# Routing tokens to experts batch by batch: token numbers scattered into fixed ranges of a table in memory, read back by one gather

## What is computed

```python
x = x + attn(cond(x, itok))        # a linear map chosen per batch, then causal attention with 16 heads of 16
h = cond2(x, itok)                 # two linear layers with relu and low-rank terms, per batch
gate_weights = softmax(h @ gate_w + gate_b, axis=-1)         # 8 experts
topk_vals, topk_idx = top_k(gate_weights, 2)
e = gelu(h @ w1[n] + b1[n]); e = gelu(e @ w2[n] + b2[n]); expert_out[n] = e @ w3[n] + b3[n]
out = x + sum over the two chosen n of topk_vals * expert_out[n]
```

## Time and profile before

| | us |
|---|---|
| median of 3 runs | 1474.47 (1473.1 to 1475.62) |
| the profiled execution | 1473.53 |
| its span, first to last instruction | 1471.8 |
| TensorE busy | 1299.8 (88%) |
| VectorE (DVE) busy | 814.7 (55%) |
| ScalarE (ACT) busy | 682.5 (46%) |
| GpSimd (POOL) busy | 515.0 (35%) |
| mean granted clock of TensorE | 0.940 of full |

### The profile page before, as it was taken

The page is one execution under the profiler, slowest core; times in us unless marked ns, Lnnn a source line. Parts: engine busy times, 40 slices in busy tenths (PEclk is TensorE's granted clock), DMA queues, the critical chain, the costliest instruction groups (busy, mean ns, idle before and its releaser), DMA issues.

```text
span 1471.8 us, 26713 instructions
## 1 busy us (share of the span) xinstructions
PE 1299.8 (88%) x8313; PEld 974.7 (66%) x8314; DVE 814.7 (55%) x1753; ACT 682.5 (46%) x1301; POOL 515.0 (35%) x809
## 2 busy tenths in 40 slices
PE   5878989988988988989989885459899999999997
PEld 3436656656656656656666554448788888888886
DVE  4626646646646646556556433745455555555553
ACT  4654654655655655655655630023333333333332
POOL 0332332332332432432332420324354444544442
PEclk9579999999999999999999978569999999999998
DMA  5112223222232132132132223733525224242220
GB/s 176 44 48 89 83 77 116 79 85 96 80 123 87 64 122 82 65 123 87 55 113 79 80 86 129 292 137 73 217 43 155 36 43 141 52 148 38 38 43 11
DMA packets 50765, 137.54 MB, mean 93 GB/s; under 512 B 10658, under 2 KB 29730, under 8 KB 49026
## 3 DMA queue, kind: packets, MB, share of 16 engines
q0 software_dynamic: 28992, 68.35, 16.4%
q1 hardware_dynamic: 21698, 68.18, 12.8%
HBM read 86.03 MB, written 51.38 MB: 93 GB/s over the span
## 4 chain that ended last, share of the span: by engine, by line
PE 71%; DVE 11%; ACT 8%; DMA 3%; issue 3%; POOL 3%; SPq 0%; POOLq 0%; DVEq 0%; ACTq 0%
PE bank L691 65%; PE bank L973 4%; DVE nmax L1359 4%; ACT q_sb L1160 3%; ACT probs_t L1153 2%; PE bank L965 1%; DVE hid_low L1286 1%; DMA xg<-hrows,gid 1%; POOL w_rest L1617 1%; ACT ot_sb L1169 1%; DMA out<-y_sb,sid 1%; POOL wsplit L1621 1%; PE bank L893 1%; DVE mm_sb L1366 1%; ACT sums L1170 1%
## 5 line engine op out<-in xcount | busy, mean ns | idle before, releaser
L1359 DVE TENSOR_REDUCE nmax<-bank 128x1 f32<-128x512 f32 (+3 forms) x512 | 221.4, 485 | 120.7 <-PE bank L691 120.4
L1153 ACT ACTIVATE probs_t<-bank 128x512 f32<-128x512 f32 (+1 forms) x384 | 181.1, 524 | 119.8 <-PE bank L691 119.3
L1193 ACT ACTIVATE g<-z 128x512 f32<-128x512 f32 x142 | 89.8, 632 | 280.6 <-DVE z L1555 280.6
L1603 POOL TENSOR_SCALAR_AFFINE_SELECT probs_t<-probs_t 128x256 f32<-128x256 f32 x256 | 97.8, 406 | 336.3 <-ACT probs_t L1153 336.1
L691 PE MATMUL bank<-wst,g1t_high 128*128 x568 | 185.7, 408 | 0.9 <-DVE g1t_low L1543 0.9
L1665 POOL DMA_INDIRECT out<-y_sb,sid x71 | 114.4, 1611 | 152.1 <-DVE y_sb L1576 69.0
L1617 POOL TENSOR_TENSOR w_rest<-w_rest,w_high 128x512 f32<-128x512 f32 x64 | 82.0, 1282 | 173.5 <-ACT w_high L1039 173.5
L1555 DVE TENSOR_TENSOR z<-bank,b_sb 128x512 f32<-128x512 f32 x142 | 98.2, 692 | 73.3 <-PE bank L691 62.6
L691 PEld LDWEIGHTS bank<-wst,g1t_high 128*128 128x128 f32 x568 | 102.6, 191 | 20.6 <-issue 1.1
L691 PE MATMUL bank<-wst,g1t_low 128*128 x284 | 113.1, 398 | 0.0
L691 PE MATMUL bank<-wst,g2t_high 128*128 x568 | 108.4, 291 | 1.5 <-DVE g2t_low L1543 1.5
(11 more groups left out here) (223 smaller groups left out, 2879.4 us busy)
## 6 DMA issues: line engine op xcount, KB each, us to landing
wst<-wsplit SPq DMA_DIRECT2D x8, 4096.0 KB, 12.5
w_rest<-in_w_all POOLq DMA_DIRECT2D x64, 256.0 KB, 2.9
wsplit<-w_high POOLq DMA_DIRECT2D x64, 256.0 KB, 2.3
wsplit<-w_rest POOLq DMA_DIRECT2D x64, 256.0 KB, 2.5
hrows<-h_sb SPq DMA_DIRECT2D x8, 528.0 KB, 4.0
x_in<-in_xT SPq DMA_DIRECT2D x8, 512.0 KB, 3.7
wb_raw<-in_lora_wb SPq DMA_DIRECT2D x8, 512.0 KB, 3.5
x1t<-in_xT SPq DMA_DIRECT2D x8, 512.0 KB, 4.3
```

What stands on the lines that cost most here:

```text
L1153: taken(nc.scalar.activation(probs_t[:, (2 * g + half) % PT_SLOTS, S * u:S * u + width], at(n, rd)[:, 0:width], ACT.Exp), n, rd)
L1193: nc.scalar.activation(g[:, :], z[:, :], ACT.Gelu).then_inc(s_g, 1)
L1359: ins = V.tensor_reduce(nmax[:, g % 2, half, i:i + 1], at(n, rd)[:, cols], AX.X, ALU.max, negate=True)
L1603: ins = nc.gpsimd.affine_select(diag, diag, [[0, 2], [1, P]], ALU.is_ge, 0.0, base=0, channel_multiplier=-1)
```

## The change

Routing is spread over the rounds. A table id_table in memory has a fixed range of 4096 places for each of the 8 experts, filled with the number 4096 (no token) at the start. In round n, DVE takes the logits of batch n - 2 (`pick`, step 24): top two, one-hot masks. TensorE counts within the batch with five matmuls (product "pre", step 26). DVE adds the running count of each expert (route_sb) and gets each token's place in the table (`give_slots`, step 27, slot_id). POOL scatters the 512 token numbers twice, for first and second choice, by eight indirect DMAs of 128 numbers of 4 bytes (`put`), three behind the load of piece 5, three behind that of 6, two behind that of 7. In round 8 slots are given for batch 6 and at its end for batch 7; their 16 puts stand at the end of the rounds. DVE computes from the counts how many tiles each expert has and which row of 128 places of the table each tile is (block_id); one indirect DMA gathers these rows (ids_t), one transpose and one copy make ids, used for gathers and scatters alike. slot_id has one buffer: DVE writes it only when all puts of the batch before have landed. The copy into logits, the one-hot products and their constants go. Every expert has at least one tile and they run in the order 0 to 7, so SP loads the weights of experts 0, 1 and 2 in round 8 (`load_run`), and the biases after them, ahead of the last hrows. `product` "pre" takes a bank of the filler ring, so the fillers after it change banks.

```diff
-HIT_GROUP = NT // 4
+CAP = B * S
+PUTS = 2 * TB
+PICK_STEP, PRE_STEP = 24, 26
+PUT_WITH = {5: (0, 3), 6: (3, 6), 7: (6, PUTS)}
...
+        if routes and step == PRE_STEP:
+            take(("pre", 0), "filler")
...
+    if not attends:
+        take(("pre", 1), "filler")
...
+    id_table = nc.dram_tensor("id_table", [NE * CAP, 1], F32, kind="Internal").ap()
...
+            def load_run(r):
+                sp.wait_ge(s_wsplit, 32 * W_PIECES * (r + 1))
+                if r >= 1:
+                    sp.wait_ge(s_w, 16 * r)
+                sp.dma_start(wst[:, (1 - r) % W_SLOTS, :, :].bitcast(F32),
+                             wsplit[r:r + 1, :, :, :].rearrange("o p h n -> (o p) h n")).then_inc(s_w, 16)
+
             def turn(rd, last=False):
+                if rd.b is None:
+                    filled(sp, ("ks", HEADS // 2 - 1), Round(rd.p))
+                    sp.dma_start(tile_sb[:, :], tile_c).then_inc(s_tile_c, 16)
+                    filled(sp, ("pv", QUADS - 1), Round(rd.p))
+                    load_run(0)
...
+                    if rd.b is None:
+                        load_run(1)
+                        for n in x1s:
+                            filled(sp, n, rd)
+                        load_run(2)
+                        filled(sp, ("h", TB - 1), rd)
+                        load_bias()
...
+            sp.dma_start(tri_f[:, :], tri).then_inc(s_const, 16)
...
+            sp.dma_start(route_sb[:, :], route_c).then_inc(s_mid, 16)
+            sp.dma_start(id_table.rearrange("(n p) o -> n (p o)", p=P), pads).then_inc(s_pads, 16)
...
-            sp.wait_ge(s_wsplit, 32 * NE * W_PIECES)
-            sp.wait_ge(s_runs, 1)
-            for r in range(NE):
-                e_run = sp.value_load(run_e[0:1, r:r + 1], min_val=0, max_val=NE - 1)
...
+            sp.wait_ge(s_ends, 1)
+            for r in range(W_SLOTS, NE):
+                v_end = sp.value_load(run_end[0:1, r - W_SLOTS:r - W_SLOTS + 1], min_val=0, max_val=TILES)
+                v_out = sp.snap(v_end + before_c[BL3])
+                sp.wait_ge(full[BL3], v_out)
+                sp.sem_inc(s_tick, 1)
+                load_run(r)
...
+                elif what == "pre":
+                    vacant(pe, n, rd)
+                    pe.wait_ge(s_hots, (p if m else rd.routed) + 1)
+                    mm(dst()[:, 0:TB * NE], tri_b[:, :], hots[:, :, :].rearrange("p t e -> p (t e)"),
+                       start=True, stop=False, skip_group_check=True)
+                    for t in range(TB):
+                        later = TB - t
+                        ins = mm(dst()[:, (t + 1) * NE:(TB + 1) * NE].rearrange("p (t e) -> p t e", e=NE),
+                                 ones_b[:, :], hots[:, t, :].unsqueeze(1).to_broadcast([P, later, NE]),
+                                 start=False, stop=(t == TB - 1), skip_group_check=True)
...
-            for n in range(2 * NT // HIT_GROUP):
-                pe.wait_ge(s_hit_r, n + 1)
-                pe.wait_ge(s_hit_v, n + 1)
-                for t in range(HIT_GROUP):
-                    ins = mm(bank[ID_BANK][:, 0:TW], hit_r[:, n % 2, t, :], hit_v[:, n % 2, t, :],
-                             start=(n == 0 and t == 0), stop=(n == 2 * NT // HIT_GROUP - 1 and t == HIT_GROUP - 1))
-                ins.then_inc(s_hitu, 1)
-
-            pe.wait_ge(s_route, 1)
+            product(Round(B), ("pre", 1))
+            pe.wait_ge(s_ids_t, 16)
+            pe.wait_ge(free[ID_BANK], before_b[ID_BANK] + 1)
+            nc.tensor.transpose(bank[ID_BANK][:, 0:TW], ids_t[0:TW, :], id_f[0:TW, 0:TW]).then_inc(full[ID_BANK], 1)
...
+                        nc.scalar.copy(tri_b[:, :], tri_f[:, :])
...
+            def pick(q):
+
+                dve.wait_ge(s_gchain, q * 3 + 1)
+                weight = route_sb[:, 0:NE].unsqueeze(1).to_broadcast([P, TB, NE])
+                for c, (src, most) in enumerate(((glog, gmax), (lg2, top))):
+                    if c == 1:
+                        link(V.tensor_reduce(top[:, :], lg2[:, :, :], AX.X, ALU.max))
+                    link(V.tensor_tensor(rk[:, c, :, :], src[:, :, :], over_e(most[:, :]), ALU.is_equal))
+                    link(V.tensor_tensor(rk[:, c, :, :], rk[:, c, :, :], weight, ALU.mult))
+                    link(V.tensor_reduce(top[:, :], rk[:, c, :, :], AX.X, ALU.max))
+                    link(V.tensor_tensor(hot[:, c, :, :], rk[:, c, :, :], over_e(top[:, :]), ALU.is_equal))
+                    if c == 0:
+                        link(V.scalar_tensor_tensor(lg2[:, :, :], hot[:, 0, :, :], -BIG, glog[:, :, :], ALU.mult, ALU.add))
+                V.tensor_tensor(hots[:, :, :], hot[:, 0, :, :], hot[:, 1, :, :], ALU.add).then_inc(s_hots, 1)
+
+            def give_slots(rd, m):
+
+                n, q = ("pre", m), rd.p if m else rd.routed
+                filled(dve, n, rd)
+                begun = route_sb[:, NE:2 * NE]
+                link(V.tensor_tensor(pre[:, :, :], at(n, rd)[:, 0:TB * NE].rearrange("p (t e) -> p t e", e=NE),
+                                     begun.unsqueeze(1).to_broadcast([P, TB, NE]), ALU.add))
+                taken(V.tensor_tensor(begun, begun, at(n, rd)[:, TB * NE:(TB + 1) * NE], ALU.add), n, rd)
+                drained(dve, n, rd)
+                link(V.tensor_tensor(rk[:, :, :, :], hot[:, :, :, :],
+                                     pre[:, :, :].unsqueeze(1).to_broadcast([P, 2, TB, NE]), ALU.mult))
+                link(V.tensor_reduce(slot[:, :, :], rk[:, :, :, :], AX.X, ALU.add))
+                if q:
+                    dve.wait_ge(s_id_put, 16 * PUTS * q)
+                V.tensor_copy(slot_id[:, :, :], slot[:, :, :]).then_inc(s_put, 1)
...
-                    V.tensor_copy(logits[:, bass.ds(p * TB, TB), :], glog[:, :, :])
...
+                if b is None:
+                    pick(p)
                 if p is not None:
                     for n_fill, piece in rd.fillers(STEPS - 1):
                         take(rd, n_fill, piece)
+                if b is None:
+                    give_slots(rd, 1)
...
+            V.tensor_scalar(block_id[:, :], block_f[:, :], own, None, ALU.add).then_inc(s_block, 1)
...
+            V.tensor_copy(ids[:, :], bank[ID_BANK][:, 0:TILES]).then_inc(free[ID_BANK], 1)
...
+            def put(q, first, last):
+
+                if q < 0:
+                    return
+                if first == 0:
+                    pool.wait_ge(s_put, q + 1)
+                    if q == 0:
+                        pool.wait_ge(s_pads, 16)
+                for i in range(first, last):
+                    t, c = divmod(i, 2)
+                    nc.gpsimd.indirect_dma_start(
+                        id_table, bass.IndirectOffsetOnAxis(ap=slot_id[:, c, t:t + 1], axis=0),
+                        route_sb[:, 2 * NE + q * TB + t:2 * NE + q * TB + t + 1], None,
+                        bounds_check=NE * CAP - 1, oob_is_err=False).then_inc(s_id_put, 16)
...
                     load_piece(b, piece)
+                    if piece > IN_STEPS:
+                        put(b - 2, *PUT_WITH[piece])
                     split_piece(b, piece)
...
+            for q in (B - 2, B - 1):
+                put(q, 0, PUTS)
+            pool.wait_ge(s_block, 1)
+            pool.wait_ge(s_id_put, 16 * PUTS * B)
+            nc.gpsimd.indirect_dma_start(
+                ids_t[0:TW, :], None, id_table.rearrange("(n p) o -> n (p o)", p=P),
+                bass.IndirectOffsetOnAxis(ap=block_id[0:TW, 0:1], axis=0),
+                bounds_check=NE * CAP // P - 1, oob_is_err=False).then_inc(s_ids_t, 16)
```

More of the change, by code:

```diff
@@ L385, in build_kernel @@
+        starts = sb("starts", [1, TILES, NE - 1], F32)
+        expert_f = sb("expert_f", [1, TILES], F32)
+        turns = sb("turns", [1, 2, TILES], F32)
+        place = sb("place", [1, 2, TILES], F32)
         xg = sb("xg", [P, 2, ROW], F32)
@@ L896, in turn @@
                         product(rd, n_fill, piece)
+                    if step == PRE_STEP and rd.routed is not None:
+                        product(rd, ("pre", 0))
                     if quad is not None:
@@ L1386, in turn @@
                         take(rd, n_fill, piece)
+                    if rd.routed is not None and step == PICK_STEP:
+                        pick(rd.routed)
+                    if rd.routed is not None and step == PRE_STEP + 1:
+                        give_slots(rd, 0)
                     if step in LOW_STEPS:
@@ L1499, in _ @@
[L1499 to L1503 removed]
+            link(V.tensor_scalar(past[:, :], tbase[:, 1:NE + 1], own, None, ALU.is_le))
@@ L1651, in gather @@
             def gather(j, vj1, buffer):
[L1652 removed]
+                nc.gpsimd.tensor_copy(gid[:, :], ids[:, bass.ds(j, 1)]).then_inc(s_gid, 1)
                 pool.wait_ge(s_gid, vj1)
```

344 lines of the change are left out of this document (112 added, 232 removed).

## The result

| | us |
|---|---|
| changed kernel, median of 4 runs | 1511.07 (1505.58 to 1515.7) |
| before, 4 runs beside them | 1475.05 (1473.1 to 1476.27) |
| ratio | 1.0232, 95% interval 1.0204 to 1.0259: slower |
| profiled execution, its span | 1511.56, 1509.8 |

The prediction was 1451 with a range of 1436 to 1467, and 0.08 for slower.

What follows compares the result with a forecast made beforehand. TensorE, busy 88% of the span, was held up by a 66.0 us stretch without overlap before the expert stage. 1473.5 - 25.8 (tail) + 3.6 (rounds) = 1451.3, about 1451 us; range 1436 to 1467.

Steps and rivals of the forecast that it cites:

- The hole and its place: Between last gate (904.60) and first transpose of gathered rows (970.57), 66.0 us without overlap, which the change should shorten.
- The price of a put on POOL: POOL's time per put, c: taken as 1.61 us, between 1.07 and 2.46, plus 0.85 once a group.
- The landing of the puts: End of the rounds: batch 6's puts land 4.1 us after issue beside loads, batch 7's 2.05 us.
- POOL in the rounds: Openings of rounds: three puts take 5.7 us against piece 5's slack of 6.68 or 3.91; load 6 late, + 1.5 us.
- The rest of the rounds: TensorE's five matmuls + 2.4 us, dropped logits copy - 0.6, ScalarE's tri cast and SP's constants at the start + 0.3.
- The bound of 0 for TensorE's five matmuls: Rounds 2 to 7: lower bound if TensorE waits nearby anyway; 0.4 us each taken, upper bound 0.6.
- The early weight load: Round 8: first weight load beside POOL's last pieces delays them, but TensorE can run ahead in eight banks; 0 taken, bound 3.
- The tail: Behind the last softmax: new chain brings tile 0's gathered rows at 944.8 instead of 970.57, 25.8 us gained.
- (d): Openings: puts hold POOL, load 6 reaches ScalarE late; slower, 1494; turns at 2.3 us per put, or above 2.6; chance 0.08.
- the lock of the shared port: Openings: DVE's casts of q_sb and k_sb would keep POOL from writing DMA descriptors, holding puts; one store came 2.61 us late.
- (b): Rival for the puts: as cheap as the gather or overlapping in the queue; rounds lose 1 to 2; 1439; chance 0.20.
- (a): The forecast itself: puts about 1.6 us (1.3 to 2.0), tail gain 19 to 31, 1442 to 1461; chance 0.54.

## Why the prediction was wrong, point by point

The prediction had the span 22 us shorter, and it is 38 longer: a miss of 60. Of these, 24 arose in the rounds (27.3 lost where 3.6 were reckoned), 22 in the last round up to its last h copy (63.2 us from batch 6's hrows, 40.9 before, reckoned as unchanged), and 12 behind that copy; nearly 4 stood already at the first hrows, and the expert stage gave 1 back.

- **The hole and its place**: right. The prediction's chain ran in the order foretold: two groups of puts, table gather, ids, first tile.
- **The price of a put on POOL**, "I take c = 1.61": too dear. It was 0.97 and 0.30 between two, 1.27. Sixteen puts cost POOL 5 us less than reckoned, which hid part of the next error.
- **The landing of the puts**, "+ 4.1" and "+ 2.05": this step failed. Both were taken from gathers of whole rows of 1 KB. They measured 19.2 and 6.10, 19.2 us more together. I had bounded what a put costs its engine from both sides, and given its landing a single value from a transfer of another shape and direction. With places 16 bytes apart the last group lands in 2.19 us, so the 2.05 was right for writes that don't neighbour each other; the group beside the loads takes 6.7 (935.21 to 941.89) where 4.1 were taken.
- **POOL in the rounds**, "+ 1.5": this step failed, and cost most: 27 us. The slack of piece 5 was compared with the time that POOL issues, and that comparison held: POOL still had 2.68 us of slack behind three puts. I listed "the split, its stores, the next load" behind the puts, but only in POOL's instruction order, and let the stores land as before. Load 6 waits until they have landed, and that wait grew from 2.33 to 8.53 us. Whether their place behind the puts in POOL's queue does it is not shown; transfers in SyncE's queue were late too.
- **The rest of the rounds**, "2.4 - 0.6 + 0.3": 0 within 2 us by the run without puts, whose rounds are those of before (633.1 and 635.1) with all of this work in. The bound of 0 for TensorE's five matmuls was the nearer end.
- **The early weight load**, "I take nothing; bound 3": this step failed too. Loads alone made the last round 9.2 longer than without (49.0), and with the puts 14.0 (57.5 to 71.5). "TensorE has eight banks to run ahead in" was no cover: in the run without puts it waited 7.10 us for hid_low.
- **The tail.** From the last h copy to the first gathered transpose I expected 44.6 us instead of 70.3; it took 56.2, so 14.2 were gained where 25.8 were promised. With places 16 bytes apart and batch 6 early it took 33.2 (920.79 to 953.95).
- **The rivals.** (d) had place, chain and sign: load 6, ScalarE's order, 1494. Its cause was wrong, and so was its turning point: the run went slower with c at 1.27, far under the 2.3 at which (d) was to decide. That its chain came true was luck as far as the first link goes. The gap that I had set beside the lock of the shared port, a store 2.61 late, came in the run without puts too (2.88 at 550.36), but no put was held: none of the 64 was busy over 1.42 us, and those issued while DVE cast q_sb (at 462.92, 690.29 and 691.60) took 1.02, 1.00 and 0.97. I had also carried a rule too far. The Trainium skill, SBUF — State Buffer, section "SBUF: two separate sides", has a DVE cast take the shared port only when its operands meet conditions, and its example copies from SBUF to SBUF; q_sb is cast from a PSUM bank, so the one late store can't be claimed for that rule, and its cause stays open. (b), cheap puts, 1439, agrees with the run without any puts (1438.61) by chance: that run has no puts to pay for, and pays 9 us for the early loads instead. The edges of (a), 1442 and 1461, are 3 to 4 us wider than its own sum gives with 3.6 lost (1446 and 1458).

## What to carry to other kernels

A DMA has three prices: what the issuing engine pays, when it lands, and what it does to the transfers under way beside it, in its own queue and in others; the third can exceed the others many times, and is read from the wait of a neighbour that has nothing to do with it. When an engine's slack is compared with what is added, the landing of its own transfers belongs in the sum, and not only the time that it issues. Before many small elements are scattered, look whether they fall next to each other; if so, spread the places (here 16 bytes apart for values of 4) and read with a stride. Before moving a transfer to a better time, ask what makes it slow: moving slow puts gave back 27 us of the 36 lost, and spreading them 48.

## What the runs showed of the hardware

- Scattered 4-byte writes are slow when their places neighbour each other: eight scatters of 128 took 6.10 us to land after the last issue at 4 bytes' distance, 3.25 at 8, 2.19 at 16, 2.13 at 64, and 2.23 as rows of 512 bytes. Beside the weight and bias loads the compact ones took 19.2, and those 16 bytes apart 6.7.
- The Trainium skill, DMA: Bandwidth & Descriptors, section "Specifications", says that writes under 512 bytes are made by reading, changing and writing back. By size alone 4-byte writes would then be equally slow at every distance; the runs disagree: 6.10 us at a distance of 4 bytes, and 2.13 at 64, where rows of 512 bytes take 2.23. That neighbours must wait for each other's turn at such a unit would fit, but no run shows the step itself; this stays open, as does why the times at 8 bytes differ so widely from run to run.
- Compact puts hold up other transfers: POOL waited 8.53 us instead of 2.33 for its 256 KB stores; hrows, in SyncE's queue, landed after 8.5 us in the median instead of 4.0 (4.1 without puts); between 970 and 980 us the DMA engines were full at 180 GB/s, with 16 KB packets that took up to 5.0 us. But the last 6 us before the last puts landed show no busy DMA engine at all, so the busy share of the DMA engines doesn't tell when writes are done.
- An indirect scatter of 128 elements costs POOL 0.97 to 1.04 us (one of 64: 1.42) and 0.30 between two, beside DVE's casts from PSUM too; with 64 elements it is 0.90 to 0.97.
